# A fused mixing, norm and gated-MLP layer on eight cores: the input loads wait for two weight loads, and a set of early layer-norm statistics is left out

## The reference, cut to what matters

```
def attn(x):                                     # on a layer-normed x
    bound     = circ_conv(x, bind_key)           # along the channels
    hologram  = decay_matrix @ bound             # causal, d ** (t - s), along the tokens
    retrieved = circ_corr(hologram, unbind_key)
    return x + gate * retrieved

def ffn(x):                                      # on a layer-normed x
    h = silu(x @ wg.T) * (x @ wu.T)              # 1024 -> 3072, weights int32 / 127
    return h @ wd.T                              # 3072 -> 1024

x = x + layernorm(attn(layernorm(x)))
x = x + layernorm(ffn(layernorm(x)))
```

## Time and profile before

| | |
|---|---|
| median of 2 runs | 836.01 us (834.87 to 837.16) |
| profiled execution, its own time | 836.89 us |
| its span on the slowest core (core 4) | 835.3 us |
| spans of the eight cores | 831.2, 822.2, 830.2, 835.0, 835.3, 832.9, 830.5, 835.3 us |
| mean granted TensorE clock, as a share of 2.4 GHz | 0.905 to 0.912 |

### The profile page before, as it was taken

How to read it: one execution, slowest core, us unless ns; L and a number is a source line. 1 busy time by engine, 2 the same in 40 slices (tenths; PEclk the granted TensorE clock), 3 DMA queues, 4 the chain that set the end, 5 groups by cost and what they waited for, 6 DMA issues and landing times.

```text
span 835.3 us, 8520 instructions; the slowest of 8 cores (822.2 to 835.3 us)
## 1 busy us (share of the span) xinstructions
PE 676.5 (81%) x3030; PEld 298.2 (36%) x3030; DVE 262.3 (31%) x645; ACT 210.0 (25%) x310; POOL 29.1 (3%) x58
## 2 busy tenths in 40 slices
PE   0095989976601699799999999699999999999993
PEld 0042323432200344244444444344444444444441
DVE  0275220566557213611111122233122111112223
ACT  2033322333341411211111122423111111112222
POOL 1000000000000000000000000000000000000000
PEclk9997665999955599899999999789999999999997
DMA  8979600000003044334444201003444444400111
GB/s 195 199 249 170 113 1 1 1 0 0 1 0 51 1 64 74 66 51 75 76 77 76 50 26 51 25 27 82 95 75 77 76 76 76 76 1 26 51 51 76
DMA packets 12282, 53.41 MB, mean 64 GB/s; under 512 B 1376, under 2 KB 1376, under 8 KB 11728
## 3 DMA queue, kind: packets, MB, share of 16 engines
q0 software_dynamic: 7632, 36.08, 26.1%
q1 hardware_dynamic: 4608, 16.78, 5.8%
HBM read 80.12 MB, written 8.39 MB: 106 GB/s over the span
## 4 chain that ended last, share of the span: by engine, by line
PE 71%; DVE 11%; issue 6%; ACT 5%; DMA 5%; DVEq 0%; POOL 0%; ACTq 0%; POOLq 0%
PE pg L659 20%; PE pu L667 19%; PE pu L736 10%; PE pf L736 10%; DMA cubb<-cuT 4%; PE pb L358 4%; PE cp L236 4%; ACT t1a L433 2%; DVE sqd L412 2%; PE pt L596 2%; ACT t1a L405 2%; PE pb L353 1%; DVE x L437 1%; DVE sta L561 1%; DVE x2t L600 1%
## 5 line engine op out<-in xcount | busy, mean ns | idle before, releaser
L659 PE MATMUL pg<-x2t,wgu 128*128 128x512 bf16 x768 | 178.6, 387 | 11.8 <-DVE xw L686 6.9
L667 PE MATMUL pu<-x2t,wgu 128*128 128x512 bf16 x768 | 173.6, 379 | 0.0
L680 ACT ACTIVATE sil<-pg,z 128x512 bf16<-128x512 f32 x96 | 65.5, 687 | 244.7 <-PE pg L659 244.7
L659 PEld LDWEIGHTS pg<-x2t,wgu 128*128 128x128 bf16 x768 | 75.0, 99 | 109.7 <-issue 26.4
L667 PEld LDWEIGHTS pu<-x2t,wgu 128*128 128x128 bf16 x768 | 75.1, 98 | 90.6
L686 DVE SCALAR_TENSOR_TENSOR xw<-sil,pu 128x512 bf16<-128x512 bf16 x64 | 43.7, 688 | 169.6 <-PE pu L667 167.9
L475 PE MATMUL pr<-hc,zt 128*128 128x512 bf16 x256 | 65.8, 403 | 16.7 <-ACT t1a L405 15.8
L236 PE MATMUL cp<-cubb,cbtb 128*128 128x512 bf16 x128 | 30.2, 402 | 40.1 <-DMA cubb<-cuT 40.1
L736 PE MATMUL pf<-wdtb,xw 128*128 128x512 bf16 x256 | 57.9, 379 | 2.1 <-DVE hc L686 2.1
L736 PE MATMUL pu<-wdtb,xw 128*128 128x512 bf16 x256 | 59.4, 386 | 0.0
L686 DVE SCALAR_TENSOR_TENSOR hc<-sil,pu 128x512 bf16<-128x512 bf16 x32 | 22.0, 688 | 90.2 <-PE pu L667 90.2
(11 more groups left out here) (99 smaller groups left out, 457.2 us busy)
## 6 DMA issues: line engine op xcount, KB each, us to landing
wgu<-wgu POOLq DMA_DIRECT2D x48, 512.0 KB, 5.5
x<-xin SPq DMA_DIRECT2D x16, 512.0 KB, 36.3
out<-x SPq DMA_DIRECT2D x16, 512.0 KB, 2.7
wdtb<-wdt POOLq DMA_DIRECT2D x1, 6144.0 KB, 41.9
cbtb<-cbt POOLq DMA_DIRECT2D x1, 2048.0 KB, 22.9
cubb<-cuT POOLq DMA_DIRECT2D x1, 2048.0 KB, 36.1
cstf_s<-cstf POOLq DMA_DIRECT2D x1, 257.0 KB, 8.6
cstb_s<-cstb POOLq DMA_DIRECT2D x1, 128.0 KB, 8.8
```

Of the source, the lines that this page charges most:

```text
L659: pe_g[eta][c] = op("tensor", lambda e, sl=sl, c=c, d=d: e.matmul(PG[sl][:, 512 * c:512 * c + 512], WGU[sl][:, 128 * d:128 * d + 128], X2T ...
L667: pe_u[eta][c] = op("tensor", lambda e, sl=sl, c=c, d=d: e.matmul(PU[sl][:, 512 * c:512 * c + 512], WGU[sl][:, 1024 + 128 * d:1024 + 128 * ...
L680: sc_sil[eta][c] = op("scalar", lambda e, sl=sl, c=c: e.activation(SIL[sl][:, 512 * c:512 * c + 512], PG[sl][:, 512 * c:512 * c + 512], AF ...
```

## The change

It does two things. The first of the 16 loads of `X` on SyncE waits until both circulant matrices have landed (WCC at 32), and the 15 others stand behind it. And the early statistics of stage 5, with their `ln_combine`, are no longer in the program.

```diff
     ld_consts = dma("gpsimd", IDBT[:], cstb[:, 512:640], "LDC")
+    w("sync", "WCC", 32)
     for t in range(TN):
         dma("sync", X[t][:], xin[:, 1024 * t:1024 * t + 1024], f"LDX{t // 4 + 1}".replace("LDX1", "LDX"))
...
         if t >= 2:
             attn_stage3(t - 2)
-            tl = t - 2
-            if tl <= 7:
-                p2 = 12 * (tl % 2)
-                w("vector", "DV", dv_xattn[tl])
-                if tl >= 2:
-                    w("vector", "DV", agg_fin[tl - 2])
-                op("vector", lambda e, tl=tl, p2=p2: e.bn_stats(STA[:, p2:p2 + 6], X[tl][:, 0:512]))
-                stat_fin[tl] = op("vector", lambda e, tl=tl, p2=p2:
-                                  e.bn_stats(STA[:, p2 + 6:p2 + 12], X[tl][:, 512:1024]), "DV")
-                if tl >= 1:
-                    q2 = 12 * ((tl - 1) % 2)
-                    w("vector", "DV", stat_fin[tl - 1])
-                    op("vector", lambda e, tl=tl, q2=q2: e.bn_aggr(aggr_out(MV1, tl - 1), STA[:, q2:q2 + 6]))
-                    gap("vector", 64)
-                    agg_fin[tl - 1] = op("vector", lambda e, tl=tl, q2=q2:
-                                         e.bn_aggr(aggr_out(MV2, tl - 1), STA[:, q2 + 6:q2 + 12]), "DV")
         if t >= 1:
             sc_sqa[t - 1] = attn_stage2(t - 1)
         sc_cp[t] = attn_stage1(t)
     sc_sqa[TN - 1] = attn_stage2(TN - 1)
     attn_stage3(TN - 2)
     attn_stage3(TN - 1)
-    w("vector", "DV", stat_fin[7])
-    q2 = 12 * (7 % 2)
-    op("vector", lambda e, q2=q2: e.bn_aggr(aggr_out(MV1, 7), STA[:, q2:q2 + 6]))
-    gap("vector", 64)
-    fin2 = op("vector", lambda e, q2=q2: e.bn_aggr(aggr_out(MV2, 7), STA[:, q2 + 6:q2 + 12]), "DV")
-    w("vector", "DV", fin2)
-    dv_ln2a_early = ln_combine(0, 8, M1c, R2s, NB2s, fold=INV127)
```

## The result

| | before | changed |
|---|---|---|
| median | 836.11 us (8 runs) | 818.58 us (817.33 to 819.42, 9 runs) |
| ratio of the two | | 0.9794, 95% interval 0.978 to 0.9807 |
| span of the slowest core | 835.3 us (core 4) | 817.3 us (core 5) |
| other cores | 822.2 to 835.3 us | 799.3 to 816.0 us |

The forecast was 818.2 us. The changed kernel is 17.5 us or 2.1% faster. The interval excludes no change at all, but it has 2% in it (0.98), the value at which the text divided its chances, so the runs don't tell on which side of 2% the gain lies. In this and the experiments some executions were disturbed on one die; the ratios leave them out, so a median can stand above its ratio.

What follows compares the result with a forecast made beforehand. PE in the untouched MLP bounds most of the run; before it, the product behind `cuT` and the DVE-ACT retrieval loop do. Gains of 12.8 + 2.8 + 2.2 = 17.8 us from 836.01 give 818.2 us, range 810.0 to 823.5.

Steps and rivals of the forecast that it cites:

- Part one: Retrieval loop between DVE and ACT: without early statistics tiles 0 to 8 take 5.64 us each, 12.8 us less.
- Part two: End of the retrieval stage: last aggregates and early `ln_combine` leave the chain, 2.8 us less.
- Part three: Loads at the start: `cuT` lands at 33 instead of 40.1, `x` later; 2.2 us gained.
- the hand-over: Start, between weights landing and `x` loading: costs 0.5 to 2.7 us, taken as 1.5.
- what is late next: Start: statistics at 68.7, not the product at 64, set the square root, so 2.2 us of 7 are gained.
- the third rival: Loads: weights no faster alone, loads lose 3 us, 823.4, or give no gain, 820.4; chance 0.17.
- the main case: Whole kernel: the three parts come as forecast, 815.5 to 821.5 us; chance 0.60.
- The rival of faster loads: Loads at the start: faster without competition, gaining 6.1 us in place of 2.2, 814.3; chance 0.08.
- The sum: Whole kernel: 12.8 + 2.8 + 2.2 = 17.8 us less, giving 818.2 us, 2.1% less.
- The scan's clock: Scan: all eight cores get core 1's 50.3 us instead of 58.5, 810.0 us; chance 0.12.
- PE as the bound of the retrieval stage: Retrieval stage: PE stays at 1.2 GHz, 7.6 us a tile, kernel 849 us; chance 0.02.
- That the early statistics were wanted: Retrieval stage: the second set couldn't replace the early statistics, nothing gained there, 833.8 us; chance 0.01.

Runs made afterwards that it cites:

- slot: Changed kernel with the early statistics of tiles 0 to 7 put back on DVE where it waits for ACT, results overwritten: 820.91 us, ratio 0.9822.
- pool_x: Changed kernel without SyncE's wait; GpSimd's queue issues the 16 loads of x right behind the two weight loads: 814.77 us, ratio 0.973.
- stats_only: Changed kernel without SyncE's wait, so the kernel before without the early statistics, loads as before: 817.07 us, ratio 0.9771.
- warm_scan: Changed kernel with eight filler matmuls, results unread, in PE's wait in each of the scan's first three chunks: 799.63 us, ratio 0.9556.
- loads_only: Kernel before with only SyncE's wait for the two weight loads added, all statistics kept: 837.83 us, ratio 1.0003.
- four_first: Changed kernel with tiles 0 to 3 of x issued at once, the other twelve waiting for both weight loads: 823.5 us, ratio 0.983.

## Why the prediction was right, and where only its sum was

**Part one, the statistics in the loop: right in size and reason.** 12.8 us were forecast and 12.8 measured. That it was the loop and not DVE's load is shown by `slot`, which has the same work for nothing.

**Part two, the end of the stage: right.** 2.8 forecast; the next statistics start 2.8 us sooner behind the addition. The 3.1 of the table hold another 0.3 us, most of it a stall of 0.23 us inside the second set's `ln_combine`, which the timeline had before and not after.

**Part three, the loads: the step that failed is the hand-over.** The product's start (33, measured 33.55) and the turn of the bound from product to `x` were right; so was "what is late next". The 1.5 us for the hand-over and 320 GB/s from its end on were not. On core 5 `x` moved 179 GB/s from 34 to 38, and DVE got tile 12 at 64.86, not 61. These 3.9 us can be divided by an estimate from the rows of core 5: 0.5 for the product's start, 1.3 for the bytes missing from 34 to 38, 0.5 for 314 GB/s in place of 320 from 38 to 62, and 1.6 at the other end, where the engines' share is 0.33 from 62 to 63 and 0.10 from 63 to 64 before tile 12 is released, and the text had 0.3 us. The term was a gain of 2.2 us and is a loss of 1.6, on the slowest core; on the three early cores it is a gain of 1 to 2. The text's own limit, that the loads lose when `x` lands after 63.4, is what happened, and the third rival ("the wait costs what it gives", forecast 820.4 to 823.4) was right on the loads, though not for its reason: alone, the weights did come 6.6 us sooner, and the hand-over ate what that gave. `pool_x` shows the size: without the hand-over 3.8 us come. That is more than the 1.5 us of the text, because the wait also opens 1.5 us behind the last bytes of the weights (core 5: 32 to 33.5), time that the text had put into the weights' landing and that a queue fills.

Two of the text's bounds don't follow from its own figures. With the weights at 36, 2.7 us and 28 us, `x` lands at 67 and the square root is at 74.8, a loss of 3.8 and not 3.5. And the bounds of the three parts add up to 815.3 to 824.9, not to the 815.5 to 821.5 of the main case.

**The rival of faster loads** needed `cuT` at 30 and `x` at 55. `cuT` came at 33.5, and `x` moved 314 GB/s on core 5 from 38 to 62, where the earlier trace rows has 320 before.

**The sum** was right to 0.4 us by luck. What the loads lacked, 3.8 us, was made up by things that the text doesn't have: the first tile of the retrieval stage came 0.9 sooner, the MLP was 2.3 shorter, the end behind it 0.5 and the end of the retrieval stage 0.3. By the experiments it is 19.2 us for the statistics, where the text has 15.6, and nothing or a loss of 1.5 for the loads (818.58 against 817.07, with ratios whose intervals overlap), where it has a gain of 2.2. The MLP's time varies by 5 us between cores of one execution, and the slowest core of before was one of those with a long one (536.2; core 5 had 534.0 before and 533.9 after). PE's waits in the gate product for weights and for nothing that the profile shows are 2.0 us on core 4 before and none on that of `stats_only`, where the MLP is 4.4 us shorter. Why stays open.

**The scan's clock** was named as a rival for a gain, with one core's pattern for all. Two of eight cores had a faster pattern than the rest, core 7 with 44.5, 6 us better than the 50.3 reckoned with, and core 2 with 52.6; the slowest core didn't. As an event in this change it didn't happen; as a mechanism it is shown by `warm_scan`, and it is bigger than the change: 18 us.

**PE as the bound of the retrieval stage** did not come. PE's waits for `t1a` in the stage fell from 15.8 us (core 4) to 6.6 (core 5), and the pace was 5.6 us a tile on all cores. **That the early statistics were wanted** falls with `stats_only`.

## What to carry to other kernels

Work on an engine inside a loop of two engines costs its whole time at one place and nothing at another: look for where the engine already waits in that loop, and put the work there, before leaving it out. To order loads, use the order of a queue or a wait that opens while the last transfer is still under way, not a wait for its landing; here the empty engines between them cost all that the order gave (ratio 1.0003). And a short wait of PE costs more than its length where the clock falls behind it, so compare the granted clock of a stage between cores before counting its matmuls.

## What the runs showed of the hardware

**The hand-over differs between cores by place.** In the changed kernel the wait of SyncE ended at 32.6 to 33.9 us on all cores, and on core 0 the engines were at 0.96 of their time from 34 to 36, on core 1 at 0.13. Cores 0, 2 and 7 were early, and cores 1, 3 and 6 late, by 3 us; in `loads_only` it was 0 and 6 early (68.7 and 68.8) against 1 and 7 (72.7 and 72.4), and 4 (69.5) against 5 (72.7). That looks as if two neighbouring cores stood in each other's way, the first to issue winning. The five profiles with this wait have 20 pairs of neighbours, and in 19 the core whose product starts first, counted from its own beginning, has the earlier table load. It was only seen, not tried.

**The granted clock was 0.81 for a while.** That is neither 1.2 nor 2.4 GHz. On four cores of `slot` and two of `four_first` it was 0.81 in most of the product, in which these kernels don't differ from the changed one. These six cores took 33.4 to 33.9 us from the first to the last matmul of the product, all cores of the eleven other profiles, and the ten others of these two, 28.6 to 30.3. Core 5 and core 3 of `slot` in the same stretch:

```profile
50.00:60.00 10.00, 10.00 (x40) 4.16 (x39) 9.30 (x33) 2.99 (x5) 0.00 (x0) 0.81 0.99 336
```

```profile
50.00:60.00 10.00, 10.00 (x48) 4.52 (x47) 9.29 (x32) 3.58 (x6) 0.00 (x0) 1.00 1.01 328
```

40 matmuls started in place of 48. On core 5 it was 0.81 at its highest from 42 to 200, and 1.00 again from 204. It cost such a core some 4 us in the product alone (33.7 us for it against 29.7), which is why these two kernels' times stand above what their stages say.

**The scan's length isn't set by its instructions alone.** The same 128 matmuls took some 58.6, 52.6, 50.3 or 44.5 us on cores of the kernels without fillers (61 at a clock of 0.81), and 39.9 to 41.4 once PE no longer waited between chunks. The time of the program follows the slowest pattern, since in each of the nine profiles without fillers at least one of the eight cores took over 58 us.
